# Attention's value product: one burst of 13 key tiles in every second slot instead of halves of 7 and 6 in every slot

## The chip, the core and the metric

The kernel runs on one NeuronCore of a Trainium2 chip. The metric is the device time of one execution, in microseconds (us), as the median of several runs. The engines are named as in the profile: PE is TensorE's matmuls, PEld its weight loads, DVE is VectorE, ACT is ScalarE, POOL is GpSimd, SP is the engine that issues most DMAs.

## The reference, cut to what matters

A decoder layer on x of 4 x 512 tokens by 1024: a mixer, a cross attention over 1601 keys per batch, and a feed-forward block. The change touches the cross attention alone:

```python
C_q = Q @ Wq_d
C_kv = K @ Wkv_d
CqWqk = (C_q @ W_qk).reshape(b, n, H, LKV)
scores = jnp.einsum('bnhl,bkl->bhnk', CqWqk, C_kv) / jnp.sqrt(jnp.asarray(LKV, dtype=Q.dtype))
attn = jax.nn.softmax(scores, axis=-1)
V_up = (C_kv @ Wv_u).reshape(b, nkv, H, HD)
out = jnp.einsum('bhnk,bkhd->bnhd', attn, V_up)
```

There are 4 batches of 16 heads, LKV is 64, and all of it is float32.

## The kernel before, in words

Three stages run one after the other, each with its own engine programs and a barrier behind it: `mixer`, `attention` and `ffn`. In `attention` the order of the work on each engine is written out by hand, and semaphores are the only ties between engines.

The unit of attention's work is 128 query tokens of one head against all 1601 keys (13 key tiles of 128, the last padded). A head g has four units q = 0 to 3, each with one slot in the loop of `tensor()` (from L839). There are 64 heads and so 256 slots, and a last round (g = 64) that drains. Two units make a pair: pair 2g is units 0 and 1 of head g, pair 2g + 1 is units 2 and 3.

Every slot begins on TensorE with `scores(g, q)` (L789): eight matmuls of 400 or 402 columns, two passes (high and low part of the keys) over four key chunks, in two halves. The first half waits on `s_ex` until ACT has taken the first exponential of the unit before out of the same four PSUM banks, the second half until it has taken the second. Then the softmax of that unit goes its own way: DVE takes the maximum of each half (L1035) and makes the negative scaled maximum `nm` (L1039), ACT takes the two exponentials into `pr` (L924). The next unit's scores can't begin before the first of them is done.

The rest of a slot on TensorE is work on older units:

- `turn(pi, e)` (L802) transposes 128x128 pieces of `pr` into three PSUM banks `tp`, from where ACT (L894, L896) and DVE (L972) copy them to `pt`. Slots q = 1 and 3 have 12 transposes, slots q = 0 and 2 have 14.
- `project(g + 1)` (L778) in q = 1 makes the next head's queries. It waits for POOL's copy `wqs` (L1075); DVE takes its result (L961, L963).
- `output(g - 1)` (L826) in q = 3 makes a head's output out of `ot`; it waits on `s_ot`.
- `weigh(pi, part)` (L815) is the value product of a pair. Key tile t multiplies `cn[:, b, t, :]` (64 columns of weights) by 256 columns of `pt`; even tiles write PSUM partitions 0 to 63 of `po`, odd tiles 64 to 127. Part 0 has tiles 0 to 6 and part 1 tiles 7 to 12, in the next slot. The last matmul of part 1 sets `s_pv`.

`s_pv` frees `pt` for the copies of the pair after next and, for both pairs of a head, lets ACT's `out_latent` (L903) copy `po` to `ot` in slot q = 2; that sets `s_ot`, for which `output` and the first `weigh` of the next head wait. POOL and SP meanwhile prepare integer weights for the third stage: after `project` and `output` of a head, POOL does two blocks of L1093 and L1095, and at some heads also a batch's normalisation (L1088) or the split of the keys.

From here on q = 0 and 2 are called even slots, q = 1 and 3 odd slots.

Of the kernel before, what the change touches and what calls it, by code (L numbers as in the profile page):

```python
# [567 lines left out]
NKT = -(-NKV // P)  # L568
KPAD = NKT * P
HEADS = 16  # L570
NHEAD = L * HEADS
# [36 lines left out]
def attention(nc, d, kvd, raw, wint, x1, x2):  # L608

    with ExitStack() as ctx:  # L610
# [3 lines left out]
        def sem(name):  # L614
            return ctx.enter_context(nc.semaphore("b_" + name))

        T, V, S, G, Q = nc.tensor, nc.vector, nc.scalar, nc.gpsimd, nc.sync
# [7 lines left out]
        s_tr, s_pa, s_pd, s_pv, s_ot = (sem(n) for n in ("tr", "p_act", "p_dve", "pv", "ot"))  # L625
# [49 lines left out]
        def bank(ev):  # L675
            return tp[AT[ev] % 3]

        def copied(eng, pi, e):
            s = pi % 2
            if e in BY_ACT[s]:  # L680
                eng.wait_ge(s_pa, pi // 2 * PER_HEAD[0] + s * len(BY_ACT[0]) + BY_ACT[s].index(e) + 1)
            else:
                eng.wait_ge(s_pd, pi // 2 * PER_HEAD[1] + s * len(BY_DVE[0]) + BY_DVE[s].index(e) + 1)

        def bank_free(eng, ev):
            if AT[ev] >= 3:
                kind, g, e = EVENTS[AT[ev] - 3]
                if kind == "turn":
                    copied(eng, g, e)
                elif kind == "project":  # L690
                    eng.wait_ge(s_ql, g + 1)
                else:
                    eng.wait_ge(s_yo, g + 1)
# [43 lines left out]
        def tensor():  # L737
            T.wait_ge(small, 16)
            T.wait_ge(later_in, 48)

            def latent_query(n):
                b, c = n // KC, n % KC
                if c == 0 and b >= 2:
                    T.wait_ge(s_cq, b - 1)
                T.wait_ge(s_xd if n % 2 else s_xa, n // 2 + 1)
                ins = T.matmul(tp[b % 2][:, :], wqd[:, c, :], xT[n % XRING], start=(c == 0), stop=(c == KC - 1))
                if c == KC - 1:
                    ins.then_inc(s_cqp, 1)

            T.wait_ge(s_zero, 1)  # L750
            for b in range(L):
                T.wait_ge(kin[b], 32)
                for k, chunk in enumerate(CN_TURNS):
                    if b:
                        T.wait_ge(s_cn, 2 * (b - 1) + k + 1)
                    for t in chunk:
                        ins = T.transpose((tp[2], po)[k][:, (t - chunk[0]) * LAT:(t - chunk[0] + 1) * LAT],
                                          kvs[b % 2][0:LAT, t * P:(t + 1) * P], ident[0:LAT, 0:LAT])
                    ins.then_inc(s_cnp, 1)
                T.wait_ge(xin[b], 16)  # L760
                for c in range(KC):
                    n = b * KC + c
                    if n >= 4:
                        T.wait_ge(s_xd if n % 2 else s_xa, n // 2 - 1)
                    for q in range(QT):
                        ins = T.transpose(sc[:, n % 4 * 512 + q * P:n % 4 * 512 + (q + 1) * P], xn[b][:, q, c * P:(c + 1) * P], ident[:, :])
                    ins.then_inc(s_xt, 1)
                    if n >= 2:
                        latent_query(n - 2)
            for n in range(L * KC - 2, L * KC):  # L770
                latent_query(n)

            def project(g):
                ev = ("project", g, 0)
                T.wait_ge(s_wq, g + 1)
                bank_free(T, ev)
                b = g // HEADS
                T.matmul(bank(ev)[:, :], wqs[:, g % 2, :, :].rearrange("p a e -> p (a e)"), cq[:, b * NB:(b + 1) * NB],  # L778
                         start=True, stop=True).then_inc(s_q, 1)

            def scores(g, q):
                u, b = g * UNITS + q, g // HEADS
                for half in range(2):
                    if u:
                        T.wait_ge(s_ex, 2 * u - 1 + half)
                    for n in (2 * half, 2 * half + 1):
                        w = KCHUNK[n] + KCHUNK[n] % 2
                        for z, k in enumerate((kh, kl)):
                            ins = T.matmul(sc[:, SCOL[n]:SCOL[n] + w], qs[g % 2][:, q * P:(q + 1) * P],  # L789
                                           k[b % 2][:, KSTART[n]:KSTART[n] + w], start=(z == 0), stop=(z == 1))  # L790
                    ins.then_inc(s_sb if half else s_sa, 1)

            def turn(pi, e):
                ev = ("turn", pi, e)
                z, k = TURNS[e]
                bank_free(T, ev)
                u = 2 * pi + z
                T.wait_ge(s_ex, 2 * (2 * pi + 1) + 2 if k == 3 else 2 * u + 1 + (k > 0))
                n = 0
                for z in ((0, 1) if k == 3 else (z,)):  # L800
                    for c in range(4 * k, 4 * k + GROUPS[k]):
                        ins = T.transpose(bank(ev)[:, n * P:(n + 1) * P], pr[(2 * pi + z) % UNITS][:, c * P:(c + 1) * P], ident[:, :])  # L802
                        n += 1
                ins.then_inc(s_tr, 1)

            def weigh(pi, part):
                b, s = pi // 2 // HEADS, pi % 2
                if part == 0:
                    if pi >= 2:
                        T.wait_ge(s_ot, pi // 2)  # L810
                    copied(T, pi, 6)
                    copied(T, pi, 5)
                for t in (range(0, 7), range(7, NKT))[part]:
                    z = t % 2
                    ins = T.matmul(po[z * LAT:(z + 1) * LAT, s * 256:(s + 1) * 256], cn[:, b, t, :], pt[s][:, t, :],  # L815
                                   start=(t < 2), stop=(t >= NKT - 2))
                if part == 1:
                    ins.then_inc(s_pv, 1)

            def output(g):  # L820
                ev = ("output", g, 0)
                T.wait_ge(s_ot, g + 1)
                bank_free(T, ev)
                h = g % HEADS
                for q in range(QT):
                    ins = T.matmul(bank(ev)[:, q * LAT:(q + 1) * LAT], ot[:, q * P:(q + 1) * P],  # L826
                                   wv[:, h * LAT:(h + 1) * LAT], start=True, stop=True)
                ins.then_inc(s_op, 1)

            T.wait_ge(s_cq, L)  # L830
            T.wait_ge(s_cn, 2 * L)
            T.wait_ge(s_xa, L * KC // 2)
            T.wait_ge(s_xd, L * KC // 2)
            project(0)
            for g in range(NHEAD + 1):
                for q in range(UNITS):
                    if g < NHEAD:
                        if q == 0:
                            T.wait_ge(s_ql, g + 1)  # L839
                            if g % HEADS == 0:  # L840
                                T.wait_ge(s_kl, g // HEADS + 1)
                        scores(g, q)
                    if q == 0 and g:
                        for e in (3, 4, 5, 6):
                            turn(2 * g - 1, e)
                        weigh(2 * g - 2, 1)
                    if q == 1:
                        if g < NHEAD:
                            for e in (0, 1, 2):
                                turn(2 * g, e)  # L850
                        if g < NHEAD - 1:
                            project(g + 1)
                        if g:
                            weigh(2 * g - 1, 0)
                    if q == 2:
                        if g < NHEAD:
                            for e in (3, 4, 5, 6):
                                turn(2 * g, e)
                        if g:
                            weigh(2 * g - 1, 1)  # L860
                    if q == 3:
                        if g < NHEAD:
                            for e in (0, 1, 2):
                                turn(2 * g + 1, e)
                        if g:
                            output(g - 1)
                        if g < NHEAD:
                            weigh(2 * g, 0)

        def scalar():  # L870
            for dst, src in ((wqd, d["wqd"]), (wqk, d["wqk"]), (wv, d["wv"])):
# [240 lines left out]

        sync()
        tensor()
        scalar()
        vector()
# [394 lines left out]
```

## Time and profile before

| | us |
|---|---|
| median of 3 runs | 3225.28 (3217.88 to 3228.97) |
| the profiled execution, its own time | 3217.43 |
| its span | 3215.6 |
| mixer, up to the first scores of attention | 459.6 |
| attention's loop, to the last head's output | 1388.2 |
| the rest of attention and ffn | 1367.8 |

| engine | busy us over the span | share |
|---|---|---|
| PE | 2940.1 | 91% |
| PEld | 2282.4 | 71% |
| DVE | 2387.4 | 74% |
| ACT | 1530.0 | 48% |
| POOL | 1561.8 | 49% |

The share of busy time is a mean over three stages with different limits, so it says little about one change; what counts is the order and the waits in attention's loop. Matmuls are pipelined: a matmul's record lasts from its start to the modelled end of its result, so records overlap, and distances between starts tell more than durations. A float32 matmul leaves two records, so a burst of 6 tiles of L815 reads as x12 and one of 7 tiles as x14; a transpose leaves one.

### The profile page before, as it was taken

The page shows a single profiled execution, that of the slowest core. Times are in us where ns is not written, and L with a number is a line of the kernel's source. Part 1 is how long each engine was busy: PE and PEld are TensorE (multiplying, and loading weights), DVE is VectorE, ACT ScalarE, POOL GpSimd, SP SyncE. Part 2 cuts the span into 40 slices and gives each one's busy share as a digit, 9 for nine tenths or more (in the row PEclk, how much of TensorE's full clock was granted, in tenths as well). Part 3 has the DMA queues.
Part 4 walks back from the last instruction along what each step waited for, and adds up shares of the span by engine and source line. Part 5 has one row for each costly group of instructions (what it writes and reads, how often), then busy time and mean ns, then how long its engine had stood idle before and what let it go on. Part 6 is the DMA issues. An engine that isn't in the chain of part 4 may idle for free. (4 is left out here: it accounts for less than half of the span.)

```text
span 3215.6 us, 44348 instructions
## 1 busy us (share of the span) xinstructions
PE 2940.1 (91%) x16436; PEld 2282.4 (71%) x16436; DVE 2387.4 (74%) x3003; ACT 1530.0 (48%) x2459; POOL 1561.8 (49%) x808
## 2 busy tenths in 40 slices
PE   6786489999999999999999959999999699999997
PEld 3554157777777777777777748888888478888885
DVE  1627737776767667677767658999999779999998
ACT  2242225555555555555555544445444355444543
POOL 0204322320343023311332058888888288888884
PEclk9888799999999999999999979999999899999999
DMA  6304653430335013430443031222222322222221
GB/s 228 129 3 156 217 198 119 150 107 1 118 134 194 21 66 138 144 119 14 150 140 112 1 143 66 79 69 69 79 73 69 122 75 70 73 79 70 68 79 66
DMA packets 103397, 322.21 MB, mean 100 GB/s; under 512 B 11153, under 2 KB 30610, under 8 KB 103186
## 3 DMA queue, kind: packets, MB, share of 16 engines
q1 hardware_dynamic: 97890, 307.78, 28.0%
q10 hardware_dynamic: 5296, 11.60, 1.0%
q8 instruction: 134, 2.20, 0.3%
q14 instruction: 77, 0.63, 0.1%
HBM read 248.50 MB, written 70.85 MB: 99 GB/s over the span
## 5 line engine op out<-in xcount | busy, mean ns | idle before, releaser
L1035 DVE TENSOR_REDUCE b_mx<-b_sc 128x1 f32<-128x802 f32 (+1 forms) x512 | 483.9, 987 | 328.7 <-PE b_sc L789 328.6
L1349 DVE SCALAR_TENSOR_TENSOR c_acc<-c_ps,c_sd,c_acc 128x1024 f32<-128x1024 f32 x448 | 572.6, 1283 | 92.6 <-PE c_ps L1247 92.6
L1291 ACT ACTIVATE c_scaled<-c_ps,c_sgu 128x1024 f32<-128x1024 f32 x336 | 375.4, 1117 | 445.5 <-PE c_ps L1247 436.8
L924 ACT ACTIVATE b_pr<-b_sc,b_nm 128x802 f32<-128x802 f32 (+1 forms) x512 | 470.9, 925 | 157.7 <-DVE b_nm L1039 157.6
L1083 POOL TENSOR_TENSOR b_y<-b_y,b_yo 128x256 f32<-128x256 f32 x64 | 46.5, 727 | 1024.7 <-DVE b_yo L986 1024.7
L815 PE MATMUL b_po<-b_pt,b_cn 128*64 128x256 f32 x3328 | 449.9, 392 | 0.0
L1402 POOL TENSOR_TENSOR c_sum_u<-c_sum_u,c_scaled 128x1024 f32<-128x1024 f32 x168 | 404.6, 2408 | 75.3 <-ACT c_scaled L1291 74.2
L1402 POOL TENSOR_TENSOR c_sum_g<-c_sum_g,c_scaled 128x1024 f32<-128x1024 f32 x168 | 404.7, 2409 | 67.0 <-ACT c_scaled L1291 66.4
L896 ACT COPY b_pt<-b_tp 128x512 f32<-128x512 f32 x320 | 187.2, 585 | 472.1 <-PE b_tp L802 472.1
L802 PE MATMUL b_tp<-b_ident,b_pr 128*128 128x128 f32 x3328 | 408.0, 273 | 0.0
L789 PE MATMUL b_sc<-b_kh,b_qs 128*128 128x400 f32 (+1 forms) x1024 | 384.3, 375 | 10.2 <-ACT b_pr L924 8.5
L802 PEld LDWEIGHTS b_tp<-b_ident,b_pr 128*128 128x128 f32 x3328 | 377.0, 140 | 16.9 <-issue 0.4
L815 PEld LDWEIGHTS b_po<-b_pt,b_cn 128*64 128x64 f32 x3328 | 235.9, 138 | 173.4 <-issue 77.3
L789 PE MATMUL b_sc<-b_kl,b_qs 128*128 128x400 f32 (+1 forms) x1024 | 355.3, 347 | 0.0
L1349 DVE SCALAR_TENSOR_TENSOR c_sum_u<-c_ps,c_sgu,c_sum_u 128x1024 f32<-128x1024 f32 x224 | 285.8, 1276 | 28.0 <-POOL c_sum_u L1402 25.3
L1349 DVE SCALAR_TENSOR_TENSOR c_sum_g<-c_ps,c_sgu,c_sum_g 128x1024 f32<-128x1024 f32 x224 | 286.3, 1278 | 25.3 <-PE c_ps L1247 14.3
L1247 PE MATMUL c_ps<-c_xh,c_uw_int 128*128 128x512 f32 x896 | 279.4, 393 | 13.6 <-DVE c_xl L1357 7.2
L1247 PE MATMUL c_ps<-c_hh,c_dw_int 128*128 128x512 f32 x896 | 278.9, 393 | 13.5 <-POOL c_hl L1418 13.5
L972 DVE COPY b_pt<-b_tp 128x512 f32<-128x512 f32 x448 | 289.1, 681 | 2.8 <-PE b_tp L802 2.3
L789 PEld LDWEIGHTS b_sc<-b_kh,b_qs 128*128 128x128 f32 x1024 | 193.3, 189 | 121.8 <-ACT b_pr L924 61.2
L1247 PE MATMUL c_ps<-c_xl,c_uw_int 128*128 128x512 f32 x896 | 278.3, 392 | 0.0
L1247 PE MATMUL c_ps<-c_xh,c_gw_int 128*128 128x512 f32 x896 | 276.8, 390 | 1.4 <-ACT c_sum_g L1291 1.3
(185 smaller groups left out, 4484.9 us busy)
## 6 DMA issues: line engine op xcount, KB each, us to landing
c_uw_int<-wint_u SPq DMA_DIRECT2D x56, 512.0 KB, 3.4
c_gw_int<-wint_g SPq DMA_DIRECT2D x56, 512.0 KB, 3.4
c_dw_int<-wint_d SPq DMA_DIRECT2D x56, 512.0 KB, 3.4
a_cx<-in_b_ctxT SPq DMA_DIRECT2D x16, 1608.0 KB, 10.9
b_rw<-in_c_gw SPq DMA_DIRECT2D x28, 512.0 KB, 3.6
b_rz<-in_c_gz SPq DMA_DIRECT2D x28, 512.0 KB, 5.2
b_rw<-in_c_uw SPq DMA_DIRECT2D x28, 512.0 KB, 3.6
b_rz<-in_c_uz SPq DMA_DIRECT2D x28, 512.0 KB, 5.3
```

The costliest lines, as they stand in the source:

```text
L789: ins = T.matmul(sc[:, SCOL[n]:SCOL[n] + w], qs[g % 2][:, q * P:(q + 1) * P], k[b % 2][:, KSTART[n]:KSTART[n] + w], start=(z == 0), stop=( ...
L802: ins = T.transpose(bank(ev)[:, n * P:(n + 1) * P], pr[(2 * pi + z) % UNITS][:, c * P:(c + 1) * P], ident[:, :])
L815: ins = T.matmul(po[z * LAT:(z + 1) * LAT, s * 256:(s + 1) * 256], cn[:, b, t, :], pt[s][:, t, :], start=(t < 2), stop=(t >= NKT - 2))
L896: S.copy(pt[pi % 2][:, 4 * k:4 * k + 4, z * P:(z + 1) * P], bank(ev)[:, :].rearrange("p (t e) -> p t e", e=P)).then_inc(s_pa, 1)
L924: S.activation(pr[q][:, k0:k1], sc[:, lo:hi], ACT.Exp, bias=nm[:, u % 2:u % 2 + 1], scale=0.125, accum_out=den[:, g % 2, q, half:half + 1] ...
L972: V.tensor_copy(pt[pi % 2][:, 4 * k:4 * k + 4, z * P:(z + 1) * P], bank(("turn", pi, e))[:, :].rearrange("p (t e) -> p t e", e=P)).then_in ...
L1035: V.tensor_reduce(mx[:, half:half + 1], sc[:, lo:hi], AX, ALU.max).then_inc(s_mb if half else s_ma, 1)
L1083: G.tensor_tensor(yh, yh, yo[:, g % 2, :, :], ALU.add).then_inc(s_ya, 1)
L1247: ins = T.matmul(pair[slot % 4][:, b * 512:(b + 1) * 512], w[n][t % 2][:, k * P:(k + 1) * P], v[:, b * 512:(b + 1) * 512], start=(z == 0), ...
L1291: S.activation(dst[:, :], pair[SLOT[x, j] % 4][:, :], ACT.Identity, scale=scale(x, j)).then_inc(s_e, 1)
L1349: V.scalar_tensor_tensor(out=total, in0=pair[SLOT[x, j] % 4][:, :], scalar=scale(x, j), in1=total, op0=ALU.mult, op1=ALU.add).then_inc(s_a ...
L1402: G.tensor_tensor(total, total, scaled[m % 2][:, :], ALU.add).then_inc(s_add, 1)
```

## The change

`weigh` loses its two parts and runs all 13 tiles of a pair in one go. It stands where part 1 stood: pair 2g - 2 in slot q = 0, pair 2g - 1 in slot q = 2. The calls in q = 1 and q = 3, which had part 0, are gone. The waits that stood ahead of part 0 now stand ahead of the burst.

```diff
-            def weigh(pi, part):
+            def weigh(pi):
                 b, s = pi // 2 // HEADS, pi % 2
-                if part == 0:
-                    if pi >= 2:
-                        T.wait_ge(s_ot, pi // 2)
-                    copied(T, pi, 6)
-                    copied(T, pi, 5)
-                for t in (range(0, 7), range(7, NKT))[part]:
+                if pi >= 2:
+                    T.wait_ge(s_ot, pi // 2)
+                copied(T, pi, 6)
+                copied(T, pi, 5)
+                for t in range(NKT):
                     z = t % 2
...
-                if part == 1:
-                    ins.then_inc(s_pv, 1)
+                ins.then_inc(s_pv, 1)
...
                     if q == 0 and g:
                         for e in (3, 4, 5, 6):
                             turn(2 * g - 1, e)
-                        weigh(2 * g - 2, 1)
+                        weigh(2 * g - 2)
                     if q == 1:
...
-                        if g:
-                            weigh(2 * g - 1, 0)
                     if q == 2:
...
                         if g:
-                            weigh(2 * g - 1, 1)
+                            weigh(2 * g - 1)
                     if q == 3:
...
-                        if g < NHEAD:
-                            weigh(2 * g, 0)
```

No other engine's instructions change in kind, number or order.

On TensorE, in an odd slot with `project` (q = 1), from the last scores of the slot to the first of the next. Before:

```order
L789 MATMUL b_sc<-b_kl,b_qs 128x400
L802 MATMUL b_tp<-b_ident,b_pr 128x128 x12
L778 MATMUL b_tp<-b_cq,b_wqs 128x512
L815 MATMUL b_po<-b_pt,b_cn 64x256 x7
L789 MATMUL b_sc<-b_kh,b_qs 128x402
```

Now:

```order
L789 MATMUL b_sc<-b_kl,b_qs 128x400
L802 MATMUL b_tp<-b_ident,b_pr 128x128 x12
L778 MATMUL b_tp<-b_cq,b_wqs 128x512
L789 MATMUL b_sc<-b_kh,b_qs 128x402
L789 MATMUL b_sc<-b_kl,b_qs 128x402
```

The seven tiles ahead of the next scores are gone; in q = 3 it is the same with `output` in the place of `project`.

On TensorE, in an even slot, from its last scores to the first of the next. Before:

```order
L789 MATMUL b_sc<-b_kl,b_qs 128x400
L802 MATMUL b_tp<-b_ident,b_pr 128x128 x14
L815 MATMUL b_po<-b_pt,b_cn 64x256 x6
L789 MATMUL b_sc<-b_kh,b_qs 128x402
L789 MATMUL b_sc<-b_kl,b_qs 128x402
```

Now (the line of `weigh`'s matmul is L814 there):

```order
L789 MATMUL b_sc<-b_kl,b_qs 128x400
L802 MATMUL b_tp<-b_ident,b_pr 128x128 x14
L814 MATMUL b_po<-b_pt,b_cn 64x256 x13
L789 MATMUL b_sc<-b_kh,b_qs 128x402
L789 MATMUL b_sc<-b_kl,b_qs 128x402
```

The seven tiles have come here: 13 stand where 6 stood.

## Rows read from the trace of the kernel before

**Rows 1.** Windows: attention's loop; busy us (instructions) of each engine, clock, DMA.

```profile
459.60:1847.80 1388.20, 1358.05 (x9334) 1042.97 (x9334) 982.94 (x1578) 748.47 (x1547) 360.83 (x304) 0.99 0.29 100
```

**Rows 2.** Timeline, even slot of head 42: start, us, instruction, [idle before <-releaser].

```profile
1371.31 0.19 PEld L789 LDWEIGHTS b_sc<-b_kh,b_qs 128*128 128x128 f32 x1 [0.38 <-issue]
...
1372.41 1.89 DVE L1035 TENSOR_REDUCE b_mx<-b_sc 128x1 f32<-128x802 f32 x2 [2.07 <-PE b_sc L789]
...
1372.70 1.65 PEld L802 LDWEIGHTS b_tp<-b_ident,b_pr 128*128 128x128 f32 x14
1373.51 0.59 ACT L896 COPY b_pt<-b_tp 128x512 f32<-128x512 f32 x1 [2.68 <-PE b_tp L802]
...
1374.52 1.06 PEld L815 LDWEIGHTS b_po<-b_pt,b_cn 128*64 128x64 f32 x12 [0.17 <-issue]
...
1374.73 0.93 ACT L924 ACTIVATE b_pr<-b_sc,b_nm 128x802 f32<-128x802 f32 x1 [0.64 <-DVE b_nm L1039]
...
1375.96 0.19 PEld L789 LDWEIGHTS b_sc<-b_kh,b_qs 128*128 128x128 f32 x1 [0.38 <-ACT b_pr L924]
```

**Rows 3.** Timeline, the odd slot that follows, and the next head's start.

```profile
1377.39 1.43 PEld L802 LDWEIGHTS b_tp<-b_ident,b_pr 128*128 128x128 f32 x12
...
1378.92 0.30 PEld L778 LDWEIGHTS b_tp<-b_cq,b_wqs 128*128 128x128 f32 x2
...
1379.38 0.93 ACT L924 ACTIVATE b_pr<-b_sc,b_nm 128x802 f32<-128x802 f32 x1 [0.57 <-DVE b_nm L1039]
1379.98 1.49 PEld L815 LDWEIGHTS b_po<-b_pt,b_cn 128*64 128x64 f32 x14 [0.76 <-issue]
...
1380.81 0.69 DVE L963 TENSOR_TENSOR b_qs<-b_tp,b_qs 64x512 fp32r<-64x512 f32 x1
...
1381.85 0.19 PEld L789 LDWEIGHTS b_sc<-b_kh,b_qs 128*128 128x128 f32 x1 [0.39 <-issue]
...
1392.30 0.19 PEld L789 LDWEIGHTS b_sc<-b_kh,b_qs 128*128 128x128 f32 x1 [0.39 <-issue]
```

**Rows 4.** Timeline, head 0, which has no value product in its first three slots.

```profile
474.51 0.93 ACT L924 ACTIVATE b_pr<-b_sc,b_nm 128x802 f32<-128x802 f32 x1 [0.88 <-DVE b_nm L1039]
...
475.59 0.45 PE L789 MATMUL b_sc<-b_kh,b_qs 128*128 128x402 f32 x1 [1.46 <-ACT b_pr L924]
...
476.49 0.19 PEld L789 LDWEIGHTS b_sc<-b_kh,b_qs 128*128 128x128 f32 x1 [0.24 <-ACT b_pr L924]
...
477.14 1.42 PEld L802 LDWEIGHTS b_tp<-b_ident,b_pr 128*128 128x128 f32 x12
```

**Rows 5.** Timeline, TensorE at the end of the loop.

```profile
1835.07 0.19 PEld L789 LDWEIGHTS b_sc<-b_kh,b_qs 128*128 128x128 f32 x1 [0.39 <-ACT b_pr L924]
...
1840.90 1.53 PEld L802 LDWEIGHTS b_tp<-b_ident,b_pr 128*128 128x128 f32 x14 [0.38 <-issue]
1842.60 4.08 PEld L815 LDWEIGHTS b_po<-b_pt,b_cn 128*64 128x64 f32 x38 [0.17 <-issue]
```

**Rows 6.** Timeline, one of five heads whose `project` waits for POOL.

```profile
1313.48 2.08 PE L778 MATMUL b_tp<-b_cq,b_wqs 128*128 128x512 f32 x2 [3.97 <-POOL b_wqs L1075]
...
1315.48 3.40 PE L815 MATMUL b_po<-b_pt,b_cn 128*64 128x256 f32 x14
...
1318.82 0.46 PE L789 MATMUL b_sc<-b_kh,b_qs 128*128 128x402 f32 x1
```

**Rows 7.** Timeline, one of three even slots with an ACT table load.

```profile
1261.92 1.28 ACT L924 ACT_TABLE_LOAD   x1 [0.63 <-DVE b_nm L1039]
...
1264.29 0.45 PE L789 MATMUL b_sc<-b_kh,b_qs 128*128 128x402 f32 x1 [1.06 <-ACT b_pr L924]
```

**Rows 8.** Waits in attention's loop: who waited for whom, us in total, times, longest.

```profile
PE b_tp L778 <- POOL b_wqs L1075: 20.8, 5, 4.5
PEld b_sc L789 <- ACT b_pr L924: 61.2, 138, 4.2
```

## The prediction

> **What bounds the kernel now.** I read the windows first, for the stage. In attention's loop TensorE has a matmul in flight for 1358 of 1388 us and its granted clock is 0.99 of full speed, the 2.4 GHz level; DVE is busy 71% of the time [rows 1]. An engine that never rests need not be the only limit, so the timeline of one head comes next, read by distances between starts of weight loads.
>
> An even slot lasts 4.65 us, from scores to scores [rows 2]. TensorE spends it thus: 1.39 from the first scores to the first transpose, 1.82 for 14 transposes up to the value product, 1.44 for 6 tiles up to the next scores. Beside it runs a chain that no order on TensorE shortens: scores, maximum (starts 1.10 in), `nm`, first exponential (starts 3.42 in), and then the next scores may start. How soon after the exponential's start? Not seen in this slot, where the tiles end at the same moment. Head 0 shows it, because TensorE has nothing else to do there: exponential at 474.51, scores at 475.59, so 1.08 [rows 4]. **The chain is 3.42 + 1.08 = 4.50 us.** An even slot thus sits 0.15 above its chain.
>
> The odd slot lasts 5.89 us [rows 3]: 1.43 for the scores, 1.53 for 12 transposes, 1.06 for `project`, 1.87 for 7 tiles. Its exponential starts 3.42 in as well, so the chain is done at 4.50 and TensorE works 1.4 us more. In both slots TensorE is the bound, and each holds enough of it to cover the chain. The head that begins at 1371.31 ends at 1392.30: 20.99 us for two of each [rows 2, 3].
>
> **The change part by part.** It moves 7 of 13 tiles from the odd slot to the even one.
>
> *The long burst.* The two halves of the array's columns work side by side: 12 records take 1.06 and 14 records 1.49 [rows 2, 3], so the lone seventh tile adds 0.43 where a couple of tiles adds the same 0.43. At the end of the loop 38 records stand back to back and take 4.08 [rows 5]: ten tiles on the fuller half, three more couples' worth of 0.43 twice over the 1.49 of four, which gives 4.05. A burst of 13 tiles has seven on the fuller half: 1.49 + 3 x 0.43 = 2.77, and with the 0.38 from the last load to the scores behind it 3.15 us. The two bursts took 1.44 + 1.87 = 3.31, so TensorE's own work falls by 0.16 a pair.
>
> *The even slot.* Its chain (4.50) is far from its end. It costs 1.39 + 1.82 + 3.15 = 6.36 us on TensorE.
>
> *The odd slot.* TensorE's part is 1.39 + 1.53 + 1.06 = 3.98 us, less than the chain, and so the chain sets the end: 4.50 us with 0.5 us idle. Also, scores that start on the first exponential catch up with the second, and their second half waits: in head 0 the loads stop for 0.24 and the scores take 477.14 - 475.59 = 1.55 in place of 1.39 [rows 4]. That puts 0.16 on the even slot: 6.52.
>
> *Sum for a head.* 2 x (4.50 + 6.52) = 22.04 against 20.99: **1.05 us more**, over 62 heads (all but the first and last) 65 us. Put shortly: before, TensorE's 10.5 us a pair hid a chain of 4.50 twice; now 6.5 us of its work lies over one chain, where 4.5 would do, and the other has 4.0 over it.
>
> *Waits that come or go.* `weigh` now asks for `s_ot` and the copies one slot later than before, so neither ends late. The finish of a pair's product was after 6 tiles of an even slot and is now at that slot's very end, 0.4 us ahead of the next scores; ACT's `out_latent` (0.6 us) stands there ahead of ACT's first copy in the odd slot, which has to start 2.20 into a slot [rows 2]. So it is covered by more than 1 us, and the copies that wait on `s_pv` come later still. DVE's last work for `project` ends 1381.50, 5.5 into its slot [rows 3]; the next maximum is due 4.50 + 1.10 = 5.6 in. It fits by 0.1, and in the next slot, an even one, a delay of up to 2 us is hidden. No DMA moves and none is waited for in the loop.
>
> *What comes back.* (a) In five heads `project` waits for POOL, 20.8 us in all [rows 8]. POOL is tied to `output` in q = 3, and from there to `project` TensorE now takes one odd and one even slot, 11.0 in place of 10.5, and the 0.5 idle of the odd slot lies under the wait: about 1.1 each, 5.5 us. (b) In three heads ACT loads a table ahead of the exponential and scores wait 1.06 [rows 7]. That chain of 5.8 now lies under an even slot of 6.5: 1.3 each with the lag behind it, 4 us. (c) The ends. Head 0 loses its first burst, -0.5. Head 63 has two even slots and an odd one without `project`: 2 x 1.87 more and about 0.3 less, +3.4. In the drain the transposes start when the second exponential allows, and 52 records stand where 38 stood: their start moves from 7.5 after the last scores to about 6.8, their length grows by four couples, 1.7 us [rows 5]: +1. Together +4.
>
> Total: 65 - 5.5 - 4 + 4 = **+59.5 us**. The profiled execution took 3217.4, which gives 3276.9; the median of the runs shown is 7.9 higher, 3225.3, and gives 3284.8. I predict 3285.
>
> **A rule against the row.** Between the transposes and a value product the loads stop 0.17, and behind it 0.38 to 0.39 [rows 2, 3]. The Trainium skill says why (TensorEngine Tiling, Key Properties): a change of tiling mode drains TensorE. By that rule alone the change, with one burst in place of two, should make attention faster; it is the first rival.
>
> **The rivals.**
> 1. *Faster: fewer drains, and the odd slot's chain doesn't decide.* TensorE's work for a pair becomes 3.98 + 6.36 = 10.34 against 10.50, so 124 pairs save 20 us, with (a) and (b) about 27: 3198. It decides only if the odd slot ends with its matmuls, and breaks even if the chain falls below about 4.0 us. For it: DVE and ACT have nothing new to do. Against: the exponential starts 3.42 in even where DVE and ACT had been idle before [rows 2], and 1.08 was seen with TensorE waiting [rows 4]. Chance 0.03; that things just cancel 0.02.
> 2. *Slower, and more: the clock falls.* After 3.97 us of waiting `project` took 2.08 and 7 tiles 3.40 in place of 1.10 and 1.94 (the records at the 1.2 GHz level), 2.4 us in all, and the next scores were quick again [rows 6]. If the 0.5 us rests brought that on in one pair of ten, it would cost 30 us: 3315. Against: after 1.46 and 1.06 us of waiting, the scores' first record has 0.45, as fast as ever [rows 4, 7]. The Trainium skill warns of this (TensorE: Matmul & The Clock Gate, A second HAM failure mode): short rests between groups of matmuls, often enough, make the clock swing. Nothing in the rows bears that out. Chance 0.03.
> 3. *Slower, and more: ACT's `out_latent` holds the odd chain.* It waits for the burst's last tile; if that came 1 us or more later than I have it, the copy and then the exponential in q = 3 move back, some 0.5 us for each head: 30 us more, 3315. Against: 1 us of cover. Chance 0.04.
> 4. The forecast, slower by about 60: 0.88.
>
> **How the numbers follow.** A measurement of this kernel tells 0.3%, about 10 us, from no change. The forecast's unknowns: the chain of the odd slot (the head 0 slot itself gives 4.43, the even slot's full length 4.65), x 126 pairs, so -9 to +19; the burst's length, +-0.02 a pair, +-3; whether a wait of 3.4 in place of 4 us still brings the clock down, up to -12; and the median, which moves by 5. So 3264 to 3303; the two larger cases above lie outside, and so does the faster one, together 1 in 10. Faster 0.03, same 0.02, slower 0.95.
>
> **What the profile would show.** Right: slots of alternately 6.5 and 4.5 us; before every even slot's scores a wait for ACT (L924) of some 0.5 to 0.7 us where the odd slots had none; 26 loads in 2.8 us; a loop of about 1448 us in place of 1388; the two outer stages as they were; the granted clock at 0.98 or above; `nm` waiting as before. Wrong: odd slots near 4.0 (rival 1), records of 0.7 for scores (rival 2), an exponential later than 3.45 into q = 3 alone (rival 3), or an even slot well under 6.3, which would say that a long burst streams faster than the rows of the drain show.

## The result, and the profile after

The changed kernel takes 3282.3 us (median of 4 runs, 3280.4 to 3284.7), the kernel before 3223.95 in the same comparison: a ratio of 1.018, 95% interval 1.017 to 1.0195. It is slower by 58 us, where 59.5 were forecast, and 3285 for the median.

The windows of attention's loop, from the first scores to the last head's first output load, in the changed kernel (busy us and instructions of PE, PEld, DVE, ACT, POOL; clock; DMA):

```profile
459.43:1906.44 1447.01, 1358.34 (x9334) 1059.45 (x9334) 952.55 (x1578) 755.17 (x1547) 361.18 (x304) 0.99 0.28 96
```

Against [rows 1] the same 9334 matmuls are in flight for the same 1358 us, but the loop has grown from 1388.2 to 1447.0: the 58.8 us are time in which TensorE has nothing in flight. The granted clock stayed at 0.99. The rest of the span moved by 5.4 us in these two executions (3215.6 - 1388.2 = 1827.4 before, 3279.8 - 1447.0 = 1832.8 after), in stages that the change doesn't touch; the medians differ by 58.3, so the loop accounts for all of it.

The timeline of head 42, first its even slot (q = 0), then the odd slot that follows and the start of the next even one (start, us, instruction, idle before and releaser). It answers to [rows 2, 3]:

```profile
1408.37 0.19 PEld L789 LDWEIGHTS b_sc<-b_kh,b_qs 128*128 128x128 f32 x1 [0.67 <-issue]
...
1409.22 0.19 PEld L789 LDWEIGHTS b_sc<-b_kh,b_qs 128*128 128x128 f32 x1 [0.18 <-ACT b_pr L918]
...
1409.90 1.67 PEld L802 LDWEIGHTS b_tp<-b_ident,b_pr 128*128 128x128 f32 x14
...
1411.74 2.78 PEld L814 LDWEIGHTS b_po<-b_pt,b_cn 128*64 128x64 f32 x26 [0.17 <-issue]
...
1414.90 0.19 PEld L789 LDWEIGHTS b_sc<-b_kh,b_qs 128*128 128x128 f32 x1 [0.38 <-issue]
...
1416.29 1.41 PEld L802 LDWEIGHTS b_tp<-b_ident,b_pr 128*128 128x128 f32 x12
...
1417.81 0.30 PEld L778 LDWEIGHTS b_tp<-b_cq,b_wqs 128*128 128x128 f32 x2
...
1418.31 0.93 ACT L918 ACTIVATE b_pr<-b_sc,b_nm 128x802 f32<-128x802 f32 x1 [0.62 <-DVE b_nm L1033]
...
1419.38 0.19 PEld L789 LDWEIGHTS b_sc<-b_kh,b_qs 128*128 128x128 f32 x1 [1.28 <-ACT b_pr L918]
...
1420.29 0.19 PEld L789 LDWEIGHTS b_sc<-b_kh,b_qs 128*128 128x128 f32 x1 [0.25 <-ACT b_pr L918]
...
1420.96 1.67 PEld L802 LDWEIGHTS b_tp<-b_ident,b_pr 128*128 128x128 f32 x14
```

The even slot lasts 6.53 us: 1.53 for scores whose second half waits for ACT, 1.84 for the transposes, 3.16 for a burst of 26 records in 2.78. The odd slot lasts 4.48. Its exponential starts 3.41 in and the next scores 1.07 later; the loads wait for nothing else ([1.28 <-ACT b_pr]). The scores behind it take 1.58. The four slots of this head take 6.53, 4.48, 6.58 and 4.53, together 22.12; the head before it takes 22.06. Before it was 20.99 [rows 2, 3].

Who waited for whom in the loop (us in total, times, longest), lines of the scores' weight loads and matmuls and of `project`'s loads:

```profile
PEld b_sc L789 <- ACT b_pr L918: 107.8, 185, 4.2
...
PE b_sc L789 <- ACT b_pr L918: 69.0, 123, 3.9
...
PEld b_tp L778 <- POOL b_wqs L1069: 19.3, 5, 4.2
```

The matmuls' line in the kernel before:

```profile
PE b_sc L789 <- ACT b_pr L924: 8.5, 5, 3.9
```

The loads' wait for ACT has gone from 61.2 to 107.8 us [rows 8] and is found in 185 places in place of 138. The matmuls' own line says it more plainly: with nothing in flight, the scores waited for ACT 5 times before, 8.5 us in all, and now 123 times, 69.0 us in all. The 60.5 us more match the 58.8 that the loop has grown by.

### The profile page after: what moved, and what is told of

It reads as the page before. It is cut to its first block and busy times, and to the rows that moved or that the text cites. A ratio compares the mean times of both kernels' runs of the same rounds, so it can differ in the third digit from the quotient of the medians.

```text
span 3279.8 us, 44348 instructions
## 1 busy us (share of the span) xinstructions
PE 2948.3 (90%) x16436; PEld 2305.3 (70%) x16436; DVE 2357.2 (72%) x3003; ACT 1536.8 (47%) x2459; POOL 1562.7 (48%) x808
## 5 line engine op out<-in xcount | busy, mean ns | idle before, releaser
L789 PE MATMUL b_sc<-b_kh,b_qs 128*128 128x400 f32 (+1 forms) x1024 | 399.2, 390 | 70.5 <-ACT b_pr L918 69.0
L814 PE MATMUL b_po<-b_pt,b_cn 128*64 128x256 f32 x3328 | 414.0, 383 | 0.0
L789 PEld LDWEIGHTS b_sc<-b_kh,b_qs 128*128 128x128 f32 x1024 | 194.9, 190 | 203.9 <-ACT b_pr L918 107.8
L814 PEld LDWEIGHTS b_po<-b_pt,b_cn 128*64 128x64 f32 x3328 | 244.8, 137 | 132.8 <-issue 21.3
```

## The experiments

Two theories were put against each other. **Chain:** each slot lasts as long as the longer of two things, TensorE's own work in it, and the chain of scores, maxima, exponential of some 4.5 us. A move of work then costs where it fills a slot that is above its chain already, and saves nothing where the slot is down at the chain. **Burst:** 13 tiles in a row cost something of their own, by their length or by what they hold up (`po`, `pt`, `s_pv`).

This table gives, for each kernel, the four slots of head 9 from starts of its first scores in the trace, and the median time. Most heads are within 0.1 us of it (45 to 57 of 62); those with a wait for POOL or a table load are not. The ratio is to runs of the kernel before taken beside each experiment, whose medians lie between 3223.6 and 3225.3.

| kernel | q = 0 | q = 1 | q = 2 | q = 3 | head | us | ratio to before (95%) |
|---|---|---|---|---|---|---|---|
| before | 4.67 | 5.85 | 4.66 | 5.82 | 21.00 | 3224 | |
| the change | 6.49 | 4.48 | 6.55 | 4.54 | 22.06 | 3282.3 | 1.017 to 1.0195 |
| one pair (e1) | 4.67 | 4.49 | 6.59 | 5.81 | 21.56 | 3253.9 | 1.0065 to 1.0102 |
| odd bursts (e2) | 4.51 | 7.32 | 4.49 | 7.28 | 23.60 | 3377.5 | 1.0456 to 1.0487 |
| split 2 / 11 (e3) | 6.07 | 4.55 | 6.06 | 4.54 | 21.22 | 3232.3 | 1.0013 to 1.0037 |
| filler, odd slots (e4) | 6.49 | 4.48 | 6.58 | 4.55 | 22.10 | 3282.3 | 1.0155 to 1.0189 |
| filler, even slots (e5) | 6.90 | 4.48 | 6.97 | 4.55 | 22.90 | 3328.4 | 1.0301 to 1.0332 |
| before, maxima of 200 (e6) | 4.67 | 5.84 | 4.67 | 5.82 | 21.00 | 3213.0 | 0.9947 to 0.9977 |
| change, maxima of 200 (e7) | 6.49 | 3.76 | 6.56 | 3.83 | 20.64 | 3187.7 | 0.9867 to 0.99 |
| one group moved (e8) | 6.07 | 4.49 | 6.10 | 4.54 | 21.20 | 3228.4 | 1.0002 to 1.0024 |
| change, maxima of 16 (e9) | 6.49 | 3.77 | 6.55 | 3.84 | 20.65 | 3189.7 | 0.9886 to 0.9916 |
| two groups moved (e10) | 5.49 | 4.58 | 5.81 | 4.92 | 20.80 | 3214.0 | 0.9954 to 0.9978 |
| before, filler in odd slots (e11) | 4.66 | 6.19 | 4.65 | 6.12 | 21.62 | 3260.4 | 1.0098 to 1.0136 |

### e1: only one pair in one burst

```diff
                     if q == 1:
...
-                        if g:
-                            weigh(2 * g - 1, 0)
                     if q == 2:
...
-                            weigh(2 * g - 1, 1)
+                            weigh(2 * g - 1, 2)
```

Part 2 stands for all 13 tiles.

> Only the pair of units 2 and 3 is weighed in one burst (slot q = 2); the pair of units 0 and 1 keeps its halves in q = 3 and q = 0. Chain theory (a slot lasts as long as the longer of TensorE's own work in it and the chain of 4.5 us): q = 1 falls to 4.5, q = 2 rises to 6.5, q = 3 and q = 0 stay at 5.8 and 4.65, so a head takes 21.5 us and the kernel is about 29 us (0.9%) slower than before, half of the whole change. Rival, the loss comes from the late release of po or pt by the burst of units 2 and 3 (out_latent waits for it): nearly all of the 58 us is here.

30 us more than before. q = 1 fell to 4.49, q = 2 rose to 6.59, and the other two slots stayed as they were. The loss is half of the whole, so it is a matter of each pair alone; the copy of `po`, which follows only this pair's burst, has no special part.

### e2: the same bursts in the odd slots

```diff
                     if q == 1:
...
+                        if g:
+                            weigh(2 * g - 1)
...
                     if q == 3:
...
+                        if g < NHEAD:
+                            weigh(2 * g)
```

The calls in q = 0 and q = 2 are left out.

> The same 13-tile bursts, but in the odd slots q = 1 and q = 3, where the 12 transposes and project or output stand too. Chain theory: odd slots take 1.55 + 1.53 + 1.06 + 3.15 = 7.3 us, even slots have 3.2 us of TensorE work and end with the chain at 4.5; a pair takes 11.8, a head 23.6, and the kernel is about 155 us (4.8%) slower than before. Rival, the long burst itself is what costs: the same 58 us as in the change.

154 us more. The bursts are the same 26 records in 2.78 us, yet the loss is 2.6 times as large. The even slot shows the wait directly (its transposes, then the next scores, TensorE's loads only):

```profile
661.25 1.66 PEld L802 LDWEIGHTS b_tp<-b_ident,b_pr 128*128 128x128 f32 x14
664.34 0.19 PEld L789 LDWEIGHTS b_sc<-b_kh,b_qs 128*128 128x128 f32 x1 [1.43 <-ACT b_pr L919]
```

After the last transpose TensorE waits 1.43 us for ACT. What decides is beside what the burst stands, not the burst.

### e3: 2 and 11 tiles

```diff
-                for t in (range(0, 7), range(7, NKT))[part]:
+                for t in (range(0, 2), range(2, NKT))[part]:
```

> Halves of 2 and 11 tiles in place of 7 and 6. Chain theory: the odd slot has 3.98 + 0.59 = 4.57 us of TensorE work, just over the chain of 4.5, the even slot 1.39 + 1.82 + 2.72 = 5.93; a pair takes 10.5 as before, so no change, within 0.3% (at most 0.1 us a pair or 13 us more, as the scores then wait a little for the second exponential). Rival, the length of the burst costs: 11 tiles in a row should bring most of the 58 us.

8 us more (0.13% to 0.37%). The slots explain 0.22 us a head, 14 us; in the trace the heads with a wait for POOL or a table load give 9 of them back. Eleven tiles in a row bring a seventh of the loss of thirteen. The odd slot is 4.55 us, where the two limits meet.

### e4, e5 and e11: the same filler in three places

In e4 the last group of transposes of each odd slot is done twice, in e5 the same is done with a group of the even slots. e11 is e4's edit in the kernel before.

```diff
-                for z in ((0, 1) if k == 3 else (z,)):
+                for z in ((0, 1) if k == 3 else (z,) * (2 if e == 2 else 1)):
+                    n %= 4
```

In e5 it is `e == 5`.

> The changed kernel with four transposes done twice in every odd slot (same data, same place). Chain theory: they lie in the 0.5 us that TensorE waits for the exponential there, 0.47 us each, so the time is that of the change, 3282 us, within 8 us. Rival, TensorE's work sets the end of the odd slots: 126 x 0.47 = 59 us more than the change.

> The changed kernel with four transposes done twice in every even slot. Chain theory: the even slots are TensorE's, so 128 x 0.47 = 60 us more than the change, about 3342 us. Rival, something else than TensorE's work ends the even slots (the copy of po, a late s_pv): clearly less than 60 us more.

> The kernel before with the four transposes done twice in every odd slot, as in e4 on the changed kernel, where they cost nothing. Chain theory: here the odd slots are TensorE's, so 0.41 to 0.47 us each, 50 to 59 us more than before. Rival, the transposes hide in waits for banks: less than 20 us more.

512 more transposes cost nothing in the odd slots of the change (3282.3 both), 46 us in its even slots, and 36 us in the odd slots of the kernel before. The odd slot of e4, transposes up to the next scores:

```profile
684.05 1.85 PEld L803 LDWEIGHTS b_tp<-b_ident,b_pr 128*128 128x128 f32 x16
685.86 0.30 PEld L778 LDWEIGHTS b_tp<-b_cq,b_wqs 128*128 128x128 f32 x2
687.13 0.19 PEld L789 LDWEIGHTS b_sc<-b_kh,b_qs 128*128 128x128 f32 x1 [0.97 <-ACT b_pr L919]
```

The wait has shrunk from 1.28 to 0.97 and the slot is as long as ever. This is the theory's plainest sign: TensorE's work in odd slots was on the path before the change and is off it now. The prices were less than expected, 0.41 us a group in e5 and 0.30 to 0.33 in e11 against 0.47 (46 us against 60, 36 against 50 to 59): the spacing of transposes (1.52 us for 12 with what follows, 1.81 for 16) holds waits for PSUM banks that more work fills. That last cause is argued from the spacing, not tried.

### e6 and e7: a shorter chain, before and after

```diff
-                            V.tensor_reduce(mx[:, half:half + 1], sc[:, lo:hi], AX, ALU.max)
+                            V.tensor_reduce(mx[:, half:half + 1], sc[:, lo:lo + 200], AX, ALU.max)
```

Each maximum is taken over 200 keys of its half only. The exponential subtracts that number and the softmax divides it out, so the function is the same as long as no exponential overflows, which depends on the data.

> The kernel before with DVE's maxima taken over the first 200 columns of each half instead of all 802 and 799 (the number subtracted ahead of the exponential is then the maximum of 400 keys, the softmax divides it out). That shortens the chain by about 0.7 us to 3.8. Chain theory: TensorE is the bound in both slots of the kernel before, so next to nothing, 0 to 6 us less. Rival, the chain has a part in the even slots already: up to 0.15 x 128 = 19 us less.

> The same shorter maxima in the changed kernel. Chain theory: the chain of 3.8 us is now below TensorE's 3.98 in the odd slot, the wait is gone, and what is left of the change is the saved end of a burst, 10.34 a pair against 10.50: about 3200 us, 80 us less than the change and 20 to 25 us less than before. Rival, the long burst costs something of its own: the time stays above that of the kernel before.

Before, all regular slots stay as they are, 4.67 and 5.84, although the exponential now starts 2.70 in: the chain had no part in them. The time fell by 12 us all the same, where 0 to 6 were expected. In the trace the loop is 7.5 us shorter: 2.1 of it in head 0, 1.9 in the five heads with a wait for POOL, 1.8 in the three with a table load, and 1.7 in the other heads together. The rest of the 12 doesn't show in these two executions. In the changed kernel the same edit is worth 95 us, and the change then is 25 us faster than the kernel before with the same edit (3187.7 against 3213.0), 38 faster than the kernel before. The 3187.7 are 12 us less than the 3200 expected. **So with a shorter chain the loss is gone: it was the wait for the chain, and the burst alone is a gain.** The odd slot of e7:

```profile
689.25 0.19 PEld L789 LDWEIGHTS b_sc<-b_kh,b_qs 128*128 128x128 f32 x1 [0.39 <-issue]
...
691.46 0.58 ACT L890 COPY b_pt<-b_tp 128x512 f32<-128x512 f32 x1 [3.71 <-PE b_tp L802]
691.50 0.21 DVE L1033 TENSOR_SCALAR b_nm<-b_mx 128x1 f32<-128x1 f32 x1
...
691.95 0.94 ACT L918 ACTIVATE b_pr<-b_sc,b_nm 128x802 f32<-128x802 f32 x1
692.16 0.30 PEld L778 LDWEIGHTS b_tp<-b_cq,b_wqs 128*128 128x128 f32 x2
...
693.02 0.19 PEld L789 LDWEIGHTS b_sc<-b_kh,b_qs 128*128 128x128 f32 x1 [0.56 <-ACT b_pr L918]
...
693.13 0.19 PEld L789 LDWEIGHTS b_sc<-b_kl,b_qs 128*128 128x128 f32 x1
```

It lasts 3.77, less than the 3.98 that TensorE was said to need there. The prediction's 3.98 is therefore too large. The scores start 1.07 after the exponential, as a slot that the chain ends would have it; whether TensorE would have been ready sooner, this run doesn't say.

### e9: is TensorE's part of the odd slot 3.8 or 3.5?

As e7, with `lo + 16`.

> The changed kernel with maxima over the first 16 columns of each half: the chain falls from 3.77 to about 3.55. In the run with 200 columns the odd slot still ended with the chain, which says that TensorE's own part there is less than the 3.98 of the prediction. New reading: next to the value product project took 1.06 because the product's mode came behind it, next to scores it takes about 0.56, so TensorE's part is 3.5: the odd slots follow the chain to 3.55, some 25 us less than with 200 columns, about 3162 us. Rival, TensorE's part is 3.8 (only 0.2 of the 1.06 goes): the time stays within 5 us of 3188.

Nothing moved, as the rival said, but the run can't tell the two apart. `nm` came 0.19 earlier and the exponential did not, since ACT has its copy of the first group ahead of it (2.70 in, in both runs; in the rows of e7 above, the copy ends when the exponential starts). ACT sets a floor of 2.70 + 1.07 = 3.77 that I had not seen, so the time would be the same with a part of 3.8 and with one of 3.5. e10 answers the question.

### e8 and e10: moving transposes instead

e8 moves one group of four transposes of each pair from its even slot to the start of the next odd slot; ACT copies it ahead of the exponential. e10 moves two, and gives the copies of the pair's first two groups to DVE. The places that depend on the order of the transposes are changed with them: the bank order in `ring_events`, the order of the copies on ACT and DVE, and the copy that `weigh` waits for. The core of e10:

```diff
-TURNS = [(0, 0), (0, 1), (0, 2), (1, 0), (1, 1), (1, 2), (0, 3)]
-BY_ACT = [(0, 2, 3, 6), (0, 3, 6)]
-BY_DVE = [(1, 4, 5), (1, 2, 4, 5)]
+TURNS = [(0, 0), (0, 1), (0, 2), (1, 0), (0, 3), (1, 1), (1, 2)]
+BY_ACT = [(2, 3, 4, 5, 6), (2, 3, 4, 5, 6)]
+BY_DVE = [(0, 1), (0, 1)]
...
                     if q == 0 and g:
-                        for e in (3, 4, 5, 6):
+                        for e in (3, 4):
                             turn(2 * g - 1, e)
...
                     if q == 1:
+                        if g:
+                            for e in (5, 6):
+                                turn(2 * g - 1, e)
```

> The changed kernel with one group of four transposes of every pair moved from its even slot to the start of the next odd slot, its copy given to ACT ahead of the exponential. Chain theory: the odd slot has 3.98 + 0.47 = 4.45 us of TensorE work, level with the chain, the even slot 1.39 to 1.55 + 1.35 + 3.15 = 5.9 to 6.05; a pair takes 10.4 to 10.55, so 3205 to 3228 us, the time of before or a little less. Rival, ACT's second early copy pushes the exponential back by 0.2 to 0.4 us: 3240 to 3270 us.

> The changed kernel with two groups of four transposes of every pair moved from its even slot to the next odd slot, both copied by ACT ahead of the exponential, and the copies of the pair's first two groups given to DVE; full maxima, same result as before. If TensorE's part of the odd slot is 3.5, it becomes 4.4 to 4.6 with 20 transposes (a wait for DVE's copy ahead of project included), level with the chain of 4.5; the even slot has 1.55 + 0.75 + 0.2 + 3.15, about 5.5 to 5.65; a pair takes 10.05 to 10.2 against 10.5 before: 3170 to 3190 us, faster than both kernels. If the part is 3.98, the odd slot is 4.9 and a pair takes 10.4 to 10.55: no better than before, 3210 to 3230 us.

e8 all but gets the time of before back (3228.4, 0.02% to 0.24% above it, at the upper edge of what was expected): the odd slot takes 16 transposes in the same 4.49 us, the even one falls by 0.43. ACT's second early copy doesn't push the exponential.

e10 is the version that **beats both kernels**: 3214.0 us, 0.22% to 0.46% under the kernel before and 2.1% under the change, with full maxima and so the same function. The expectation had two branches: 3170 to 3190 if TensorE's part of the change's odd slot is 3.5 us, 3210 to 3230 if it is 3.98. The time lies in the second, 24 us above the first. The q = 1 slot:

```profile
676.40 2.36 PEld L806 LDWEIGHTS b_tp<-b_ident,b_pr 128*128 128x128 f32 x20
...
678.25 1.28 DVE L976 COPY b_pt<-b_tp 128x512 f32<-128x512 f32 x2
678.42 0.93 ACT L928 ACTIVATE b_pr<-b_sc,b_nm 128x802 f32<-128x802 f32 x1
679.04 0.30 PEld L782 LDWEIGHTS b_tp<-b_cq,b_wqs 128*128 128x128 f32 x2 [0.28 <-issue]
679.07 1.10 PE L782 MATMUL b_tp<-b_cq,b_wqs 128*128 128x512 f32 x2
...
679.58 0.19 PEld L793 LDWEIGHTS b_sc<-b_kh,b_qs 128*128 128x128 f32 x1 [0.24 <-ACT b_pr L928]
679.61 0.74 PE L793 MATMUL b_sc<-b_kh,b_qs 128*128 128x402 f32 x1
680.01 0.19 PEld L793 LDWEIGHTS b_sc<-b_kl,b_qs 128*128 128x128 f32 x1 [0.24 <-issue]
...
681.30 0.76 PEld L806 LDWEIGHTS b_tp<-b_ident,b_pr 128*128 128x128 f32 x6
681.66 1.89 DVE L1039 TENSOR_REDUCE b_mx<-b_sc 128x1 f32<-128x802 f32 x2
```

From `project`'s first load to the scores' first load it is 0.54 us, which looks like the part of 3.5. But that load runs ahead: `project`'s matmuls are in flight until 680.17, the scores' first matmul takes 0.74 in place of 0.45, and the next load stops for 0.24 and starts 0.43 after the first, not 0.11 as elsewhere. The scores of q = 2 then last 1.72 in place of 1.40, although they wait for no exponential in there. The steadier measure is the distance from `project`'s first load to the scores' second: 0.97 us in e10, and 0.97 in e7 (692.16 to 693.13) and e9 too. Less the usual 0.11, `project` takes 0.86 next to scores. **TensorE's own part of the change's odd slot is thus 1.40 + 1.51 + 0.86 = 3.77 us**; with `output`, which takes 0.89 up to the scores in e10, it is 3.80. That is e9's rival, and it means that in e7 and e9 TensorE and ACT reach the end of the odd slot at almost the same moment.

The gap to the first branch follows. In both odd slots TensorE waits 0.28 ahead of `project` or `output`, whose bank is freed by the first of the two DVE copies that start at 678.25 (they take 1.28 together, so the first ends at about 678.9). With that wait, q = 1 holds 1.40 + 2.64 + 0.86 = 4.90 us of TensorE's time, of which 0.32 is paid in the slot behind, and q = 3 lasts 4.92. Both lie 0.4 above the chain, where the first branch had them level with it.

## Why the prediction was right, point by point

- **What bounds the kernel.** Right. e6 shows that the chain had no part in the regular slots before, e11 that TensorE's work did.
- **The chain of 4.50.** Right: the odd slots are 4.48 and 4.54. In the change's q = 3 the scores follow the exponential by 1.13 in place of 1.07; why is open.
- **The long burst.** Right: 26 loads take 2.78 and 3.16 up to the scores, against 2.77 and 3.15. Its length is right; what is saved by leaving out the other burst was put at 0.16 a pair and is more: e7 is 0.16 a pair under e6 although the scores in its even slots take 1.52 to 1.57 in place of 1.40, behind the second exponential (see the wrong term below).
- **The even slot** of 6.52: 6.50 and 6.57. The scores' wait for the second exponential is there (1.53 and 1.58).
- **The sum for a head**, 1.05: it is 1.06 to 1.13, 1.09 in the median head.
- **The waits that come and go.** `out_latent` is as described. In the timeline of the change it starts 0.1 into the odd slot, and ACT's first copy there follows 2.2 in, 1.5 us after `out_latent` has ended:

```profile
1425.96 0.19 PEld L789 LDWEIGHTS b_sc<-b_kh,b_qs 128*128 128x128 f32 x1 [0.39 <-issue]
1426.06 0.59 ACT L897 COPY b_ot<-b_po 128x512 f32<-128x512 f32 x1 [1.09 <-PE b_po L814]
...
1428.16 0.59 ACT L890 COPY b_pt<-b_tp 128x512 f32<-128x512 f32 x1 [1.51 <-PE b_tp L802]
```

- **What comes back.** The five heads with a wait for POOL were 33 us above the others before and are 25 above them now: 8 us back, where I had 5.5. The size was off because in one of the five the clock did not fall, which the range had allowed for. The heads with a table load gave back all of theirs, as said. The loop's total is +58.8, forecast +59.5. That it is so close is in part luck: the heads cost some 2.5 us more than forecast, and the wait for POOL gave as much more back.
- **One term was wrong and cost nothing: TensorE's part of the odd slot.** I took `project`'s 1.06 from a slot in which the value product followed, and kept it when the product was gone. Next to scores it is 0.86 [e10], so the part is 3.77 and not 3.98. As both are below 4.50 the sum didn't feel it; only the wait in an odd slot is 4.48 - 3.77 = 0.7 us in place of 0.5. Rival 1 did feel it: its saving was put at 0.16 a pair and 20 us, and by this count TensorE's work falls by 0.36 a pair, some 45 us (an estimate: 10.50 less 3.78 + 6.36, for 124 pairs). e7 is 25 us under e6; its even slots still hold the scores' wait for the second exponential. The rival's break-even stands: with an even slot of 6.53 a pair is back at 10.50 when the odd slot lasts 3.97. The two drains that the Trainium skill's rule (TensorEngine Tiling, Key Properties) speaks of were read from the idle time of the loads, 0.17 ahead of a product and 0.38 behind it. The runs fit a drain ahead of the product also in the odd slots, but there it hides in the work before: `project` takes 1.06 up to a product and 0.86 up to scores, `output` 1.03 and 0.89. That the drain is the reason is argued, not tried.
- **Rival 2**, a falling clock, did not come: 0.99 in the loop as before. By the Trainium skill's warning on short rests between groups (TensorE: Matmul & The Clock Gate, A second HAM failure mode) it might have; with rests of this size no run here shows it. **Rival 3** had its 1 us of cover; its sign, an exponential later than 3.45 into q = 3, isn't there (3.41), and e1 spoke against it too.

## What to carry to other kernels

When work is moved between stretches that each have to cover a chain on other engines, write down for every stretch two numbers, the engine's own work and the chain, and take the larger: evenly spread work hid the chain twice, lumped work hid it once. A filler of known size, put once in each kind of stretch, tells in two runs which of the two numbers holds there, and how much room is left. A duration read next to one neighbour is not the duration next to another: where the neighbour is removed, look for a place in the trace that lacks it. And a distance to the next step's first load can be too short, since that load may run ahead of its matmul; the distance to the second load shows it.

## What the runs showed of the hardware that I had not expected

After waits of the same length TensorE's clock fell in one head and not in another. In the kernel before, a wait for POOL of 3.9 to 4.5 us was followed in all five heads by a stretch at the lower level, 1.2 GHz. In the change two heads waited for the same time, 3.45 and 3.44 us (the timeline of TensorE, `project` and the scores' first matmul behind it, in heads 39 and 55):

```profile
1349.57 2.08 PE L778 MATMUL b_tp<-b_cq,b_wqs 128*128 128x512 f32 x2 [3.45 <-POOL b_wqs L1069]
1350.65 1.32 PE L789 MATMUL b_sc<-b_kh,b_qs 128*128 128x402 f32 x1
...
1708.86 1.12 PE L778 MATMUL b_tp<-b_cq,b_wqs 128*128 128x512 f32 x2 [3.44 <-POOL b_wqs L1069]
1709.42 0.75 PE L789 MATMUL b_sc<-b_kh,b_qs 128*128 128x402 f32 x1
```

In the 2 us from `project`'s start the granted clock was 0.50 in the first and 1.00 in the second. `project` took 2.08 and the head 27.6 us in the first, 1.12 and 24.8 in the second: 2.8 us of difference, and the clock is the only one that the rows show. In e4 three heads waited 3.00 us each; `project` then took 2.08 twice and 1.13 once. The short waits in some 126 odd slots (1.28 us between loads in the rows of head 42) brought no fall: the granted clock of the loop is 0.99, as before.

Also new to me: a weight load can start while the matmul ahead of it still streams, even when that hides for a moment what the matmul costs. In e10's q = 1 the scores' first load starts 0.54 us after `project`'s first, and their second one 0.97 after it, exactly as in e7, where the first starts at 0.86.
